# Two-layer transformer block: masked keys' stand-ins taken from the context, and the second layer's keys projected last

## What is computed

```python
# layer 0: cross attention to the context, no mask; then a feed forward with 32 experts in 4 sets
x = x + tanh(g_xattn[0]) * attention0(layernorm(x), ctx, ctx)
x = x + tanh(g_ffn[0])   * experts(layernorm(x))
# layer 1: cross attention with biases and a mask over keys; then another feed forward
k = ctx @ Wk.T + bk;  v = ctx @ Wv.T + bv           # 16 heads of 32
scores = q k / sqrt(32); scores = where(mask == 0, -1e30, scores)
x = x + tanh(g_xattn[1]) * (softmax(scores) v @ Wo.T + bo)
x = x + tanh(g_ffn[1])   * ffn(layernorm(x))
```

## Time and profile before

| | |
|---|---|
| median of 3 runs | 1455.13 us (1452.8 to 1456.88) |
| the profiled execution, its own time | 1455.15 us |
| its span in the trace | 1453.4 us |
| granted TensorE clock, mean | 0.964 |
| busy: PE, DVE, ACT, POOL | 1312.2, 900.5, 570.3, 476.5 us (90, 62, 39, 33%) |
| first `max_rows` (L1475) starts | 145.04 us |

### The profile page before, as it was taken

How to read it: one execution, slowest core, us unless ns; L and a number is a source line. 1 busy time by engine, 2 the same in 40 slices (tenths; PEclk the granted TensorE clock), 3 DMA queues, 4 the chain that set the end, 5 groups by cost and what they waited for, 6 DMA issues and landing times.

```text
span 1453.4 us, 28336 instructions
## 1 busy us (share of the span) xinstructions
PE 1312.2 (90%) x10624; PEld 939.5 (65%) x10624; DVE 900.5 (62%) x1572; ACT 570.3 (39%) x1029; POOL 476.5 (33%) x380
## 2 busy tenths in 40 slices
PE   7967899999999979886989999999996799999997
PEld 5745567777777667622446666765764577777776
DVE  5788266656666546554545655656663577777762
ACT  3321544344434445443452342343243433333331
POOL 3744335432441100000441321331130644444450
PEclk9988899999999989998999999999998899999999
DMA  9944342444223566999883552463302311111100
GB/s 338 327 153 133 94 142 74 117 165 157 86 85 122 189 182 190 341 394 366 321 335 99 173 172 74 155 201 98 129 23 88 116 42 59 59 59 59 59 32 36
DMA packets 128853, 219.56 MB, mean 151 GB/s; under 512 B 27286, under 2 KB 48278, under 8 KB 124686
## 3 DMA queue, kind: packets, MB, share of 16 engines
q1 hardware_dynamic: 128782, 218.58, 44.4%
HBM read 135.67 MB, written 82.88 MB: 150 GB/s over the span
## 4 chain that ended last, share of the span: by engine, by line
PE 47%; issue 22%; DVE 10%; DMA 6%; ACT 6%; POOL 6%; SPq 2%; POOLq 0%; DVEq 0%; ACTq 0%
PE b L152 8%; PE b L154 7%; PE b L153 7%; PE b L1494 3%; PE b L1666 3%; PE b L1943 3%; PE b L1667 3%; PE b L1668 2%; DVE f_mix L2158 2%; PE b L1976 2%; PE b L1587 2%; PE b L1466 2%; PE b L1596 2%; ACT e_gt L1862 2%; ACT a_pr L1102 2%
## 5 line engine op out<-in xcount | busy, mean ns | idle before, releaser
L1102 ACT ACTIVATE a_pr<-b 120x512 f32<-120x512 f32 x256 | 133.9, 602 | 124.9 <-PE b L1494 124.9
L1270 DVE TENSOR_REDUCE a_mx<-b 128x4 f32<-128x480 f32 x256 | 151.5, 650 | 4.6 <-PE b L1466 4.5
L1040 POOL TENSOR_TENSOR a_atl<-a_pvs,a_ath 128x512 fp32r<-128x512 f32 x64 | 81.1, 1291 | 196.8 <-ACT a_ath L1150 196.8
L999 POOL TENSOR_TENSOR a_rstd<-a_ve,a_mhalf 128x4 f32<-128x4 f32 x16 | 16.2, 1012 | 321.8 <-DVE a_ve L1219 321.8
L1666 PE MATMUL b<-a_woh,a_ath 128*128 128x512 f32 x256 | 105.8, 413 | 3.6 <-POOL a_atl L1040 3.6
L152 PE MATMUL b<-a_xth,a_wqh 128*128 128x512 f32 x256 | 104.1, 407 | 0.0
L1668 PE MATMUL b<-a_woh,a_atl 128*128 128x512 f32 x256 | 102.3, 399 | 0.0
L1667 PE MATMUL b<-a_wol,a_ath 128*128 128x512 f32 x256 | 102.2, 399 | 0.0
L154 PE MATMUL b<-a_xth,a_wql 128*128 128x512 f32 x256 | 101.9, 398 | 0.0
L153 PE MATMUL b<-a_xtl,a_wqh 128*128 128x512 f32 x256 | 101.8, 398 | 0.0
L1392 DVE SCALAR_TENSOR_TENSOR a_x<-b,a_gate,a_x 128x512 f32 (+1 forms) x64 | 47.8, 746 | 85.5 <-PE b L1668 85.5
(11 more groups left out here) (219 smaller groups left out, 3267.9 us busy)
## 6 DMA issues: line engine op xcount, KB each, us to landing
a_rp<-s_rp SPq DMA_DIRECT2D x128, 256.0 KB, 4.5
s_x<-a_x SPq DMA_DIRECT2D x16, 1024.0 KB, 4.2
s_rp<-e_chosen SPq DMA_DIRECT2D x16, 1024.0 KB, 7.7
s_rp<-e_xc SPq DMA_DIRECT2D x16, 1024.0 KB, 7.3
kv_xb<-in_x SPq DMA_DIRECT2D x8, 1024.0 KB, 9.5
a_xr<-in_x_t SPq DMA_DIRECT2D x8, 1024.0 KB, 6.3
a_x<-in_x SPq DMA_DIRECT2D x8, 1024.0 KB, 8.4
s_xn<-a_xn SPq DMA_DIRECT2D x8, 1024.0 KB, 4.8
```

The source lines that it names most:

```text
L1040: pool.tensor_tensor(atl[:, g], pvs[:, g], f(ath[:, g]), ALU.subtract).then_inc(a_lo, 1)
L1102: act.activation(pr[:, h % RING, :], bank[k][0:S2, :], ACT.Exp, scale=SCALE)\
L1270: dve.tensor_reduce(mx[:, t, :, r], bank[k][:, 0:HJ * S2].rearrange("p (a s) -> p a s", a=HJ), AX.X, ALU.max).then_inc(free[k], 1)
```

## The change

1. **Stand-ins once, from the context.** The mean of kept keys of a linear projection is the projection of the mean of kept context rows. So `craw` (kept in a buffer of its own) is changed in place: POOL multiplies each of its 4 chunks by `held` (L281 after units 9, 10, 12, 13), DVE takes the means (L402, L403 after units 11, 12, 14, 15) and fills masked rows (L407, 8 instructions of 128x120 for each chunk, after units 16 to 19). After unit 23, ACT casts `ch` anew (L329) and DVE `cl` (L418). A layer 1 key unit is then evicted like one of layer 0, with its bias: ACT L321 and DVE L388.
2. **Order of units.** Layer 0 keys, layer 0 values, layer 1 values (16 to 23), layer 1 keys (24 to 31).
3. **Queries and maxima among the last units.** The first batch's queries stand behind units 23, 24 and 26, and two maxima tiles behind each unit from 24 to 31. Their banks alternate between two that the units don't use.
4. **Moves that go with it.** `norm(j)` now stands behind every fourth unit (the last, `norm(7)`, behind unit 29, where it was behind 22), `first_norm` of batch 0 at 15 and 17 on POOL, its casts at 18 and 20, its low parts at 20 and 21; `wql` and `wcl` at 19; the mask tables at 6 (were at 12). `first_norm_high(act, 1)` moves from turn 0 to unit 30 on ACT. On SP the load of the layer 1 key weights stands behind x 1, the mask and the biases, x's loads at every fourth unit, and the first keys' load at 17, the second x at 23.

The diff, cut to its core:

```diff
+QUERIES_AFTER = {23: (0, 1), 24: (2,), 26: (3,)}
+MAXIMA_AFTER = {n: ((n - 24) // 2, (0, 1) if n % 2 == 0 else (2, 3)) for n in range(24, 32)}
...
-    units = [(0, "k", u) for u in range(8)] + [(0, "v", u) for u in range(8)] + [(1, "k", 0), (1, "k", 1)]
-    for u in range(2, 8):
-        units += [(1, "k", u), (1, "v", u - 2)]
-    units += [(1, "v", 6), (1, "v", 7)]
-    SPLITS = {3: 1, 9: 2, 14: 3}
-    NORMED, NORMED_HIGH, NORMED_LOW = {12: (0, 1), 14: (2, 3)}, {18: (0, 1), 20: (2, 3)}, {19: (0, 1), 21: (2, 3)}
+    units = [(lay, kind, u) for lay, kind in ((0, "k"), (0, "v"), (1, "v"), (1, "k")) for u in range(8)]
+    SPLITS, MASKS = {3: 1, 11: 3, 19: 2}, 6
+    KEPT, MEANS, FILLS, RENEW = {9: 0, 10: 1, 12: 2, 13: 3}, {11: 0, 12: 1, 14: 2, 15: 3}, {16: 0, 17: 1, 18: 2, 19: 3}, 23
+    NORMED, NORMED_HIGH, NORMED_LOW = {15: (0, 1), 17: (2, 3)}, {18: (0, 1), 20: (2, 3)}, {20: (0, 1), 21: (2, 3)}
...
+            if n in KEPT:
+                c = KEPT[n]
+                pool.wait_ge(held_done, 1)
+                pool.wait_ge(lo_done, C + c + 1)
+                pool.tensor_tensor(craw[:, c], craw[:, c], held[:, :], ALU.mult).then_inc(kept, 1)
...
+            if n == RENEW:
+                act.wait_ge(full[n % NB], n // NB + 1)
+                for c in range(C):
+                    act.wait_ge(filled, c + 1)
+                    act.activation(ch[:, c], craw[:, c], ACT.Copy).then_inc(new_hi, 1)
+            following.begin_act(act, n)
...
-            dve.wait_ge(kept_done, u + 1)
-            steps.link(dve.tensor_reduce(mean[:, u % 2], by_batch(kept[:, k]), AX.X, ALU.add))
-            steps.link(dve.tensor_tensor(mean[:, u % 2], mean[:, u % 2], share[:, half * 4:half * 4 + 4], ALU.mult))
-            steps.link(dve.tensor_tensor(by_batch(fill[:, :]), by_batch(dropped[:, half * HALF:(half + 1) * HALF]),
-                                         mean[:, u % 2].unsqueeze(2).broadcast_to([P, B // 2, S2]), ALU.mult))
-            dve.tensor_tensor(kept[:, k], kept[:, k], fill[:, :], ALU.add).then_inc(k_new, 1)
...
+                if lay:
+                    dve.scalar_tensor_tensor(out=kl[:, k, :], in0=src[:, 0:HALF], scalar=bk[:, u // 2:u // 2 + 1],
+                                             in1=f(kh[:, k, :]), op0=ALU.add, op1=ALU.subtract).then_inc(k_lo, 1)
...
+            if n in MEANS:
+                c = MEANS[n]
+                dve.wait_ge(kept, c + 1)
+                steps.link(dve.tensor_reduce(mean[:, c], craw[:, c].rearrange("p (b s) -> p b s", s=S2), AX.X, ALU.add))
+                steps.link(dve.tensor_tensor(mean[:, c], mean[:, c], share[:, :], ALU.mult))
+            if n in FILLS:
+                c = FILLS[n]
+                for b in range(B):
+                    ins = dve.scalar_tensor_tensor(out=craw[:, c, of_batch(b)], in0=dropped[:, of_batch(b)],
+                                                   scalar=mean[:, c, b:b + 1], in1=craw[:, c, of_batch(b)],
+                                                   op0=ALU.mult, op1=ALU.add)
+                ins.then_inc(filled, 1)
...
+        def begin(act, n):
+
+            if n == 22:
+                act.wait_ge(c_in, 16 * 4)
+                act.activation(gate[:, :], gate[:, :], ACT.Tanh).then_inc(gated, 1)
+            if n in QUERIES_AFTER:
+                queries(None, QUERIES_AFTER[n])
+            if n == 30:
+                first_norm_high(act, 1)
...
-            if route and first_turn(i):
-                first_norm_high(act, 1)
...
+        def begin(pe, n):
+
+            if n == 23:
+                pe.wait_ge(w_lo[0], C)
+            if n in MAXIMA_AFTER:
+                if n == 24:
+                    pe.wait_ge(kbd_in, 16 * HJ)
+                r, ts = MAXIMA_AFTER[n]
+                for t in ts:
+                    max_tile(None, 0, r, t)
+            for m in QUERIES_AFTER.get(n, ()):
+                queries(None, m)
```

More of the change, by code:

```diff
@@ L172, in keys_and_values @@
     wh, wl = [a for a, _ in w_hl], [a for _, a in w_hl]
[L173 to L177, removed]
+    raw = [sb.over(f"kv_raw{i}", [P, C, D], f"kv_wl{i}") for i in range(3)]
+    ch, cl, craw = sb("kv_ch", [P, C, N], F32R), sb("kv_cl", [P, C, N], F32R), sb("kv_craw", [P, C, N])
+    held, dropped = sb("kv_held", [P, N]), sb("kv_dropped", [P, N])
     kh, kl = sb("kv_kh", [P, NK, HALF], F32R), sb("kv_kl", [P, NK, HALF], F32R)
@@ L281, in sync @@
                 following.load_weights(sp)
-            if n == 18:
+            if n == 17:
                 for b in range(NK):
@@ L481, in tensor @@
                 cols = slice(half * HALF, (half + 1) * HALF)
+                ready = None
+                if not n:
+                    ready = lambda c: pe.wait_ge(lo_done, C + c + 1)
+                elif lay and not u:
+                    ready = lambda c: pe.wait_ge(new_lo, c + 1)
                 last = three_passes(
@@ L842, in max_bank @@
     def max_bank(i, r, t):
-        if merge and i is None:
+        if i is None:
             k, uses = MT[t % 2]
@@ L1086, in choices_out @@
                .then_inc(free["t"], 1)
+        def begin(act, n):
[6 more added lines that the diff above has]
+                first_norm_high(act, 1)
+        if route and step_of is not None:
+            return begin(act, step_of)
         if route:
-            act.wait_ge(c_in, 16 * 4)
-            act.activation(gate[:, :], gate[:, :], ACT.Tanh).then_inc(gated, 1)
-            queries(None, range(C))
             negated_max(None)
@@ L1264, in queries, with maxima @@
                 ins.then_inc(free[k], 1)
-        def maxima(i, r):
-            for t in range(NT):
+        def maxima(i, r, ts=range(NT)):
+            for t in ts:
                 k, use = max_bank(i, r, t)
@@ L1271, in maxima, with begin @@
                                   AX.X, ALU.max).then_inc(free[k], 1)
[L1273 to L1284 removed]
+        def begin(dve, n):
+            if n == 22:
+                steps = Steps(dve, dchain)
+                dve.wait_ge(const, 1)
+                steps.link(dve.tensor_reduce(part[:, :], ident[:, :].rearrange("p (a b) -> p b a", b=2)[:, 1, :], AX.X,
+                                             ALU.add))
+                steps.link(dve.tensor_scalar(part[:, :], part[:, :], -1.0, None, ALU.mult))
+                dve.wait_ge(c_in, 16 * 4)
+                dve.wait_ge(gated, 1)
+            if n in MAXIMA_AFTER:
+                maxima(None, *MAXIMA_AFTER[n])
+            if n in QUERIES_AFTER:
+                queries(0, QUERIES_AFTER[n])
+        if route and step_of is not None:
+            return begin(dve, step_of)
         def behind(dve, p):
```

217 lines of the change are left out of this document (78 added, 139 removed).

## The result

The changed kernel takes 1463.42 us (median of 6 runs, 1460.52 to 1465.57) against 1455.16 for the kernel before (6 runs); the ratio is 1.0058 with the interval 1.0042 to 1.0074. It is slower by 8.3 us, outside what counts as no change here (0.3%), and 0.6 us from the forecast of 1464. The profiled execution has a span of 1461.7 us.

A forecast was written before the change was run, and what follows sets the result against it. Before the first maxima rows (145.04 us) PE waits and DVE sets the pace. Rows at 144.9 plus 10.9 (Term B) give 155.8; less 145.04 and 2.2 (Turn 0), +8.6 on 1455.15: forecast 1464, range 1451 to 1471.

The forecast's parts named there:

- The sum: Whole execution: 155.8 - 145.04 - 2.2 = +8.6 us on 1455.15, giving 1463.8, forecast 1464.
- the stand: PE idle before unit 23, from 80.7 to 94.2 us, waiting for unit 19's eviction by DVE: 13.5 us.
- Term B: ACT's queue at unit 30: unit 31's cast waits behind second-batch casts needing POOL's eight operations after norm(7); 10.9 us.
- Turn 0: First turn after the maxima rows: loses four ACT casts from between its exponentials, -2.2 us.
- Term A: Behind norm(4), DVE gets one two-input instruction per POOL operation; unit 19 evicted at 94.1 where 83 was possible.
- The ceiling: PE's work packed at full clock before the maxima rows would end at 115.6 us, 29.4 us before 145.04.
- The fill: One DVE fill of 128x120 masked keys: 0.2 us, with bounds 0.08 and 0.64.
- The key units: After unit 24: seven units, two queries and 16 tiles take 27.7 us; norm(6) and norm(7) add 5.4.
- short fills slip between POOL's operations: Rival: several short DVE fills go between two POOL operations, unit 19 evicted at 79.6; 1449.5 us, chance 0.10.
- The case between: Rival: some fills slip, or Term B is shorter because norm(7) runs earlier; 1452 to 1459 us, chance 0.14.
- The worse case: Rival: x batch or value weights land after DVE's 57 us, or fills cost 0.4; 1469 to 1472, chance 0.12.
- The case in which all promised came true: Rival: DVE keeps ahead and PE is packed, Term A and Term B both gone; 1424 us, chance 0.02.

The follow-up runs named there:

- e_batch1_first: The change, with POOL normalising the second batch right behind norm(6)'s power, ahead of the wait for norm(7); 1453.0 us, ratio 0.9987.
- e_pool_halves: The change, with POOL's four operations on chunks 2 and 3 and its four for wql each cut into two of half the columns; 1464.8 us, ratio 1.0087.
- e_fills_late: The change, with chunks 2 and 3 filled behind units 20 and 21 instead of 18 and 19; 1464.8 us, ratio 1.0064.
- v_norm7_last: e_batch1_first with norm(7) behind the last unit's maxima on DVE and its power last on POOL; 1449.1 us, ratio 0.9976.
- v_act_fills: v_norm7_last with the tables of means, fills, first_norm and wql moved, ACT making the fills' products and DVE only adding them; 1440.2 us, ratio 0.9916.
- e_no_wql: The change, with POOL writing zeros for the low parts of the query and expert weights instead of computing them; 1456.9 us, ratio 1.0031.

## Why the prediction was right

**The sum** was +8.6 us at the second turn, and it measured +8.57. The rows were +11.0 for +10.8, turn 0 -2.4 for -2.2. Part of that exactness is luck: the stand was 11.2 us for 13.5, turn 0 came out right for a wrong reason, and a query at the lower clock, for which the forecast had nothing, was made up for by POOL's shorter operations.

**Term B** was right in mechanism and near in size. 10.9 us were forecast; the two kernels without it have their first rows 8.7 and 9.7 us sooner (9.3 each, counted from the end of their unit 31). Unit 31 ended 1.3 us later than worked out and POOL was 1.1 quicker (12.0 us for eight operations where I put 13.1). But its price was not only that wait: behind it the start of turn 0 runs at a granted 0.67, and turn 0 takes 45.2 us where it takes 41.96 in `e_batch1_first`. At the second turn term B costs some 13 us in all (9.7 and 45.21 - 41.96 = 3.3), and the prediction had nothing for the second part. The medians of the change and `e_batch1_first` are 10.4 us apart.

**Turn 0.** The step "turn 0 loses the four casts, 2.18 us, -2.2" gave the right number (47.63 to 45.21, -2.4) for a wrong reason. The casts are worth 1.1 us. The rest is that the kernel before also ran part of its turn 0 at the lower clock, which cost it 4.6 us where the change lost 3.3: with the casts at the same place and the clock at 1.00 the turn takes 43.07. Of the 4.6, 2.9 are lost in the first 20 us (granted 0.80 in the first 16) and 1.6 behind them, in a second stretch at the lower clock:

```profile
165.04:169.04 4.00, 4.00 (x43) 2.25 (x43) 1.54 (x3) 0.60 (x1) 0.81 (x1) 0.57 1.12 317
```

**Term A** was right in what happens: one two-input DVE instruction for each POOL operation, PE standing before unit 23 until 94 (forecast 94.2, measured 93.86), and `e_pool_halves` shows the turns directly. The stand itself was 11.24 us for the 13.5 forecast, since unit 22, behind a wait of 2.8 us, ran at a granted 0.67 and ended at 82.6 for 80.7. It was wrong in the ledger, where the sentence "The ceiling's 29 us have gone into ... the stand and its slow restart (15.9)" makes PE's stand the cost. `e_fills_late` removed 9.6 of its 11.2 us and unit 24 came 1.6 us sooner. The cost is DVE's way from 57 us to the end of the new `cl`: its own work, plus most of POOL's piece (7.2 us at the fills and 3.2 at the low parts, of 13.4). The three edits that rearranged this piece moved the end of unit 24 by no more than 1.6 us. That the position of unit 24 came out right (109.8) is because I had laid out DVE's list too, and that list, not PE's, set it.

**The fill** was taken at 0.2 us and is 0.26; with POOL's operations shorter than taken (1.56 for 1.64 us beside fills, 13.4 for 15.1 for all nine) nothing was left of that at unit 19.

**The key units** came at the forecast price: 2.11 us of wait for each of `norm(6)` and `norm(7)`, and the slower tiles behind each wait, make the 2.7 that `v_norm7_last` shows for the second. What the forecast lacked is the fourth query at the lower clock, 4.50 us for 2.96, which is why unit 31 was 1.3 us late.

**The rivals.** That short fills slip between POOL's operations is refuted: they took 9.32 us for eight. The case between, 1452 to 1459, lies below all 6 runs. The worse case asked for loads that land later than the 57 us taken for DVE, and DVE was free at 56.2. The case in which all promised came true needed A and B gone; `v_act_fills` is some way towards it, with rows at 132.7 against a ceiling of 115.6.

## What to carry to other kernels

Before moving a cast or an eviction ahead on an engine that executes in order, follow its input back to its last producer: here it hung on a norm on DVE and eight operations on POOL that no one else needed yet, and moving POOL's part ahead of that wait made the same order good. Where DVE's two-input instructions and POOL's operations share a stretch, count the two engines' times as one sum on the path; rearranging inside the stretch mostly moved the waits here. What shortened it was work taken off POOL (`e_no_wql`) and, in `v_act_fills`, work taken off DVE together with tables that put it where POOL has less to read. A large wait of the bounding engine is not yet a cost: look whether the engine it waits for is busy all the way to the next meeting point, and cost that engine's path.
